# Expert layers: slots filled from one-hot products, token rows gathered tile by tile, shared tiles run beside the routing

## The reference, cut to what matters

```python
# expert layer 1 (F = 1024, 8 experts, best 2, with biases; the input rows are normalised first)
xn     = layernorm(x) * gamma + beta
probs  = softmax(xn @ Wr + br)
topv, topi = top_k(probs, 2)
moe    = sum over the two experts of  topv * (relu(xn @ W1[e] + b1[e]) @ W2[e] + b2[e])
# expert layer 2 (F = 512, 8 experts, best 2, no biases, weights renormalised) plus a shared expert for all tokens
probs  = softmax(xt @ Wg);  topv, topi = top_k(probs, 2);  topv = topv / sum(topv)
moe    = sum over the two experts of  topv * (gelu(xt @ Wu[e]) @ Wd[e])
shared = gelu(xt @ W1) @ W2
```

## Time and profile before

| | |
|---|---|
| median of 3 runs | 1692.89 us (1692.78 to 1692.92) |
| the profiled execution | 1693.18 us |
| its span | 1691.3 us |
| m0, first to last instruction | 686 to 1098 us of the span |
| m1 | 1407 to 1691 us of the span |
| PE, DVE, ACT, POOL busy | 84%, 66%, 60%, 56% |

### The profile page before, as it was taken

One profiled execution on the slowest core, in us unless ns is written; L12 is line 12 of the kernel. 1 busy time (PEld: TensorE's weight loads), 2 busy tenths in 40 slices (PEclk: granted clock), 3 DMA queues, 4 the chain that ended last, 5 costly groups with the idle time before them and its releaser, 6 DMA issues. The chain is left out here.

```text
span 1691.3 us, 28713 instructions
## 1 busy us (share of the span) xinstructions
PE 1412.6 (84%) x9650; PEld 1160.2 (69%) x9650; DVE 1115.1 (66%) x2456; ACT 1013.4 (60%) x2444; POOL 944.9 (56%) x940
## 2 busy tenths in 40 slices
PE   3778999999999999574999999168899965899991
PEld 3556777777777776564999999134555535789991
DVE  3566766666666666544677777569898962666664
ACT  3666565565565565103778788357777843358883
POOL 3786554444444445054888878127677761646661
PEclk9899999999999999586999999679999995899996
DMA  4100000000005600356565654254343410357664
GB/s 137 39 26 7 26 8 8 2 7 7 2 8 138 161 1 1 108 172 205 187 240 205 242 210 167 112 171 144 128 140 120 139 49 26 111 141 245 229 220 167
DMA packets 87453, 188.33 MB, mean 111 GB/s; under 512 B 25544, under 2 KB 58256, under 8 KB 78864
## 3 DMA queue, kind: packets, MB, share of 16 engines
q1 hardware_dynamic: 79824, 165.93, 29.5%
q0 software_dynamic: 7488, 20.59, 3.4%
HBM read 151.31 MB, written 35.18 MB: 110 GB/s over the span
## 5 line engine op out<-in xcount | busy, mean ns | idle before, releaser
L301 POOL TENSOR_TENSOR a_pexp<-a_pexp,a_rsum 128x384 f32<-128x384 f32 (+1 forms) x320 | 246.1, 787 | 282.5 <-DVE a_rsum L502 282.5
L394 ACT ACTIVATE a_pexp<-a_ps,a_nmax 128x384 f32<-128x384 f32 (+1 forms) x320 | 181.3, 568 | 175.3 <-DVE a_nmax L498 175.2
L1356 PE MATMUL m_ps<-m_xT,m_w1s 128*128 128x256 f32 x1848 | 279.4, 288 | 8.3 <-POOL m_w1s L841 5.1
L1374 PE MATMUL m_ps<-m_w2s,m_hs 128*128 128x256 f32 x1848 | 270.1, 282 | 2.7 <-DVE m_hs L1241 2.7
L1356 PEld LDWEIGHTS m_ps<-m_xT,m_w1s 128*128 128x128 f32 x1848 | 245.5, 193 | 13.9 <-POOL m_w1s L841 9.8
L1374 PEld LDWEIGHTS m_ps<-m_w2s,m_hs 128*128 128x128 f32 x1848 | 240.7, 189 | 3.1 <-DVE m_hs L1241 2.9
L498 DVE TENSOR_REDUCE a_nmax<-a_ps 128x1 f32<-128x384 f32 (+1 forms) x320 | 154.1, 523 | 68.3 <-PE a_ps L592 67.2
L1594 POOL TENSOR_TENSOR s_hc<-s_h,s_bc_rows 128x1024 f32<-128x1024 f32 x64 | 151.0, 2362 | 79.9 <-DVE s_h L1836 79.6
L841 POOL TENSOR_TENSOR m_w2s<-m_w,m_w2s 128x512 fp32r<-128x512 f32 x111 | 143.9, 1297 | 90.1 <-ACT m_w2s L1031 89.5
L1836 DVE TENSOR_TENSOR_SCAN s_h<-s_dps,s_inp 128x512 f32<-128x512 f32 x128 | 149.1, 1207 | 0.0
L608 PE MATMUL a_ps<-a_ident,a_pexp 128*128 128x128 f32 x896 | 145.1, 275 | 3.4 <-ACT a_pT L255 3.0
(11 more groups left out here) (318 smaller groups left out, 3269.1 us busy)
## 6 DMA issues: line engine op xcount, KB each, us to landing
s_bc_rows<-s_bc_table SPq DMA_DIRECT2D x64, 512.0 KB, 3.7
m_w<-in_down SPq DMA_DIRECT2D x31, 1024.0 KB, 8.2
m_w<-in_up SPq DMA_DIRECT2D x23, 1024.0 KB
m_w<-in_up SPq DMA_DIRECT2D x24, 512.0 KB
m_w<-in_down SPq DMA_DIRECT2D x24, 512.0 KB
slots<-a_zero SPq DMA_DIRECT2D x2, 5980.0 KB, 39.6
m_xrow<-slots SPq DMA_DIRECT2D x46, 256.0 KB
m_w<-results SPq DMA_DIRECT2D x4, 1024.0 KB, 7.8
```

The lines of the kernel that those rows point to most:

```text
L301: nc.gpsimd.tensor_tensor(pexp[:, r, 0:n], pexp[:, r, 0:n], rsum[:, r:r + 1].to_broadcast([128, n]), ALU.mult).then_inc(normed, 1)
L394: nc.scalar.activation(pexp[:, r, 0:n], ps_s[score_bank(u)][:, 0:n], ACT.Exp, bias=nmax[:, r:r + 1], accum_out=sums[:, r:r + 1]).then_inc( ...
L1356: last = nc.tensor.matmul(ps_hid[ft % RING], w1s[wb][wp][:, k, ft * 128:(ft + 1) * 128], xT[:, j % 2, xp, k, :], start=(k == 0 and wp == 0 ...
L1374: last = nc.tensor.matmul(ps_y[j % 2][:, s, :], hs[hp][:, ft % RING, s * 128:(s + 1) * 128], w2s[wb][wp][:, ft, :], start=(ft == 0 and s = ...
```

## The change

- The zero fill of the slot tables goes. Instead of `slots` there is a `table` of 2049 rows: row 0 is zero, row 1 + n is token n. SP stores the tokens' rows there by 4 plain DMAs of 4 blocks each.
- The 32 scatters go. The slot number is cut into a high digit (46 values) and a low one (128). DVE makes one-hot tables of both digits for the 32 (choice, block) pairs, and PE sums 32 products of them into the token number of every slot (`numbers_of_slots`). 64 more products give the weight of every slot (`weights_by_slot`); POOL prepares their right sides (`slot_weights`).
- The rows of a tile come by two indirect DMAs on POOL (`gather_rows`), those of tile j + 2 ahead of the other work of POOL's tile j. SP's `load_rows` goes.
- m1 starts its shared tiles right after the router scores. The routing is cut into steps that DVE does between them (`routing_step`), and PE's sums and products stand in the shared tiles 2, 6 and 7.
- m0: three of the eight constants run ahead of the sums, three between sums and products, two behind; x is doubled by ACT group by group in the routing, and the term is added by DVE in the tile loop, one block per tile.
- The chunks whose low part DVE makes are 0, 1, 2 (of 4) and 0, 3, 6 (of 8) in place of 0, 3 and 0, 4. In shared tiles ACT makes the rounded half of every hidden chunk.
- In m1 the rows of tiles 8 and 9 are transposed at step 0 of tiles 7 and 8 instead of step 2 of tiles 6 and 7.

```diff
-    on_dve = lambda c: c in (0, 3) if FT == 4 else c in (0, 4)
+    on_dve = lambda c: c in (0, 1, 2) if FT == 4 else c in (0, 3, 6)
+    high_on_act = lambda j, ft: j < TILES_SHARED or (ft % 4 in (1, 3) if FT == 4 else ft % 4 == 1)
...
+    def rows_at(j, ft):
+        if shared and ft == 0 and j + 1 in (TILES_SHARED, TILES_SHARED + 1):
+            return j + 1
+        if ft == X_STEP and j + 2 < TILES and not (shared and j + 2 in (TILES_SHARED, TILES_SHARED + 1)):
+            return j + 2
+        return None
...
 @block.sync
-                sp.wait_ge(s_scat, 16 * 2 * TT)
-                load_rows(TILES_SHARED)
-                load_rows(TILES_SHARED + 1)
+                for g in range(GROUPS):
+                    ...
+                    sp.dma_start(by_token[:, t, :], x[:, t, :] if ln_rows is None else xn_group(g)).then_inc(s_stored[g], 16)
...
 @block.gpsimd
-                for t in range(TT):
-                    for k in range(2):
-                        nc.gpsimd.indirect_dma_start(slots, ...(ap=slot_i[:, k, t:t + 1], axis=0), rows[:, t, :], None).then_inc(s_scat, 16)
+                def gather_rows(j):
+                    q, b = j - TILES_SHARED, j % 2
+                    pool.wait_ge(xT_raw, j + 1)
+                    for s in range(2):
+                        nc.gpsimd.indirect_dma_start(xrow[:, b, s, :], None, table,
+                                                     ...(ap=row_from[:, 2 * q + s:2 * q + s + 1], axis=0)).then_inc(xrow_loaded[b], 16)
...
+                if shared:
+                    slot_weights()
+                for g in range(GROUPS):
+                    pool.wait_ge(s_stored[g], 16)
+                pool.wait_ge(s_from, 1)
+                gather_rows(TILES_SHARED)
+                gather_rows(TILES_SHARED + 1)
                 if shared:
                     for c in range(FT):
                         low_part(TILES_SHARED, c)
+                else:
+                    slot_weights()
                 for j in range(TILES_SHARED, TILES):
+                    if j + 2 < TILES:
+                        gather_rows(j + 2)
                     if j == TILES_SHARED + 1:
                         destinations()
                     for c in range(FT):
                         if j + 1 < TILES:
                             low_part(j + 1, c)
                         if c == FT // 2 and j > TILES_SHARED:
                             scatter_rows(j - 1)
...
 @block.vector
+                def high_digits():
+                    link(nc.vector.tensor_tensor(high_hot[:], iota_hi..., slot_hi..., ALU.is_equal))   # 128 x 32 x 46
+                def numbers_by_high_digit():
+                    nc.vector.tensor_tensor(by_number[:], high_hot[:], value, ALU.mult).then_inc(s_by_number, 1)
+                def low_digits(c):                                                                   # 128 x 8 x 128
+                    nc.vector.tensor_tensor(low_hot[:, n, :], iota_lo..., slot_lo..., ALU.is_equal).then_inc(s_low_hot, 1)
...
 @block.tensor
+                def numbers_of_slots():
+                    pe.wait_ge(s_by_number, 1)
+                    for n in range(PAIRS):
+                        if n % (PAIRS // 4) == 0:
+                            pe.wait_ge(s_low_hot, n // (PAIRS // 4) + 1)
+                        last = nc.tensor.matmul(ps_id, low_hot[:, n, :], by_number[:, n, :], start=(n == 0), stop=(n == PAIRS - 1))
...
                 def transposes(j):
                     b, q = j % 2, j - TILES_SHARED
                     if routed(j):
-                        pe.wait_ge(xrow_loaded[b], 16 * (q // 2) + 16)
+                        pe.wait_ge(xrow_loaded[b], 32 * (q // 2) + 32)
...
+                        if shared and (j, ft) == (2, 1):
+                            count_slots()
+                        if shared and (j, ft) == (6, 1):
+                            numbers_of_slots()
+                        if (j, ft) == ((7, 1) if shared else (0, 4)):
+                            weights_by_slot()
+                        if rows_at(j, ft) is not None:
+                            transposes(rows_at(j, ft))
```

More of the change, by code:

```diff
@@ L284, in _ @@
                 for table in empty:
[L285 to L286 removed]
+                    sp.dma_start(table[0:1, :], zero[:]).then_inc(s_filled, 16)
                 sp.wait_ge(s_filled, 16 * len(empty))
@@ L1008, in take_root, with high_part @@
                     nc.scalar.activation(rstd[:, cols], rstd[:, cols], ACT.Sqrt).then_inc(s_rstd, 1)
+                W_DMAS = 3 if b_up is not None else 2
+                def high_part(weights, tile, c):
+                    n, half, wb = weights
+                    if c == 0:
+                        act_e.wait_ge(w_loaded[wb], (half + 1) * W_DMAS * 16)
+                        if tile is not None:
+                            act_e.wait_ge(h_used, tile * FT + 1)
+                    nc.scalar.copy(chunk(c, (w1s[wb][0], w2s[wb][0])), chunk(c, (w1[:, wb], w2[:, wb]))).then_inc(w_high, 1)
                 for g in range(GROUPS):
@@ L1248, in _ @@
                 dve.sem_inc(w_low_dve, 2 * DVE_LOWS)
+                if not shared:
+                    softmax_scores()
+                    probabilities()
+                    maxima()
+                    indices(0)
+                    indices(1)
+                    choices()
+                    one_hot()
+                    counts()
+                    tile_bounds()
+                    tile_experts()
+                    ranks()
+                    slot_numbers()
+                    slot_digits()
+                    high_digits()
+                    numbers_by_high_digit()
+                    for c in range(4):
+                        low_digits(c)
+                    slot_rows()
                 for c in range(FT):
@@ L2015, in decoder @@
     rows = (TOP_K * T + E * (SLOTS - 1)) // SLOTS * SLOTS
-    slots = [nc.dram_tensor(f"slots{n}", (rows, D + 4), fp32).ap() for n in range(2)]
-    results = [nc.dram_tensor(f"results{n}", (2 * T + 2 + rows, D), fp32).ap() for n in range(2)]
+    tables = [nc.dram_tensor(f"table{n}", (T + 1, D), fp32).ap() for n in range(2)]
+    results = [nc.dram_tensor(f"results{n}", (2 * T + rows, D), fp32).ap() for n in range(2)]
     flat = lambda t: t.rearrange("a s d -> (a s) d")
@@ L2037, in decoder @@
         moe_layer(nc, sems, "m1", tokens, flat(out), a["wr1"], None, None, a["up1"], None, a["down1"], None,
-                  slots[1], results[1], ACT.Gelu, True, True)
+                  tables[1], results[1], ACT.Gelu, True, True)
 def kernel(**inputs):
```

466 lines of the change are left out of this document (283 added, 183 removed).

## The result

| | time of the device | span of the profiled execution |
|---|---|---|
| kernel before | 1692.9 us (1692.8 to 1693.8, 4 runs) | 1691.3 us |
| predicted | 1736 us, range 1698 to 1776 | |
| changed kernel | 1886.5 us (1881.0 to 1889.3, 4 runs) | 1882.7 us |

The ratio is 1.114 (95% interval 1.111 to 1.117): slower, as forecast, but by 194 us instead of 43. The range didn't hold it, nor did the dearest rival (1774).

A forecast was written before the change was run, and what follows sets the result against it. PE was taken to bound the tile loops. From 1693.2 us, m0 gave -26, m1 ahead of tile 8 gave -1 and m1's routed tiles +70.6: 1736.8, or 1736 by the median's measure, range 1698 to 1776.

The forecast's parts named there:

- the dearest rival: m1's routed tiles: landing of 3.7 us and clock lost after each stall, 1774 us in all; chance 0.15.
- The chain in m1: m1's routed tiles: transposition, up, ACT, POOL's low part, gather, transposition close a loop; period 10.5 us, +70.6 in all.
- For L I take 3.0: m1's routed tiles: L, the gather's time from second DMA's issue to landing, taken as 3.0 us; period 9.98 before clock loss.
- In m0's loop the same chain has room: m0's tile loop: gather lands at X + 9.9 (X is a transposition), within a tile of 11.8 us, so no wait.
- lost in a third of the tiles: m1's routed tiles: PE's clock drops after the stall in a third of them, adding 0.5 us to the period.
- The rival with the clock always lost: The dearest rival: m1's clock lost after each stall, L = 3.7, tiles of 12.3 us, 1774 us in all; chance 0.15.
- The thin products: PE's added products of 46 columns at 0.09 us each: 5.8 us for 64 in m0, 8.6 for 96 in m1.
- The forecast's doubt: Sign that the prediction is wrong: products of 46 columns on PE costing more than 0.19 us each.
- m1's front: m1 ahead of tile 8: earlier start against added products, routing and first gather's wait; -1 us, ends -10 and +8.
- m0's loop starts at 758.6: m0's front: the loop's first transposition moves from 783.44 to 758.6, -24.8 us, within m0's total of -26.
- Rival 3: m1's routed tiles: gather hides behind PE because POOL comes early or the wait asks less; total near 1655 us; chance 0.10.
- Rival 4: m0's loop: indirect DMAs 0.2 us longer make POOL 12.0 us a tile, 13 us more, 1750 in all; chance 0.09.

The follow-up runs named there:

- e2: Changed kernel with each weight load cut to 128 KB from the third routed tile on, gathers left in place: 1795.1 us, 1.060 of before.
- e3: Changed kernel without POOL's gathers; SP loads rows of fixed positions by plain DMAs where it loaded rows before the change: 1698.0 us, 1.003 of before.
- e1: Changed kernel with POOL gathering the rows of tile j + 3 instead of j + 2, a tile earlier: 1714.1 us, 1.012 of before.
- e11: Changed kernel with SP issuing a tile's weights only when its rows have landed: 1829.6 us, 1.054 of before on its chip.
- e10: e1 plus 92-column weight products, reordered fronts, m0's addition moved a tile later, m1's chunk 2 low part ahead of DVE's split: 1683.5 us, 0.968 of before.

## Why the prediction was wrong

- **Right: the mechanism, link by link, and the sign.** The chain in m1 is as written. Its steps, as means of 20 tiles (T2 to T22, T10 to T30), beside the 11 tiles of e2's m1 in which the clock was kept:

| step of a period | forecast | m1 | m0 | e2, clock kept |
|---|---|---|---|---|
| transposition to POOL's low part | 4.15 + 0.5 | 5.97 | 4.66 | 4.20 |
| low part to first gather | 1.44 | 1.44 | 1.61 | 1.44 |
| first gather to second | 1.29 | 1.29 | 1.30 | 1.29 |
| second gather to next transposition (L + 0.1) | 3.1 | 4.43 | 6.87 | 3.04 |
| period | 10.5 | 13.1 | 14.4 | 9.98 |

  With the landing as forecast and no slow clock the period is 9.98, the forecast's own.
- **The failed step is "For L I take 3.0".** For the second DMA L is 4.4 in m1 and 6.8 in m0. e2, with small loads, has 3.3 and 3.4; the rest is the company of the weights. The text knew that the two start together, and its own rows had the price. The median of 3.7 in the earlier trace rows mixes two kinds. The first scatter of a pair leaves ahead of the weights, the second with them. In the kernel before, for the two scatters of the earlier trace rows, at 1557.59 and at 1558.88, and with SP's issue of the weights between them:

```profile
DMA to landing us min/median/max: 2.4/2.4/2.4
```

```profile
1558.83 0.33 SPq L891 DMA_DIRECT2D m_w<-in_down  x1
```

```profile
DMA to landing us min/median/max: 5.3/5.3/5.3
```

  Over the 18 pairs in 1520:1640 the first has a median of 2.4 and the second of 5.4, with 4.3 at the least. The bytes were in sight as well, 2.25 MB per tile of m0; at the 380 to 450 GB/s of the view above they are some 5.5 us. The Trainium skill ("DMA: Bandwidth & Descriptors", the anatomy of a DMA on the gpsimd path) gives 2.3 us, an estimate for one transfer by itself; e2's second gathers in m1 took 2.7 at the least and 3.0 in the median, so the rule was low even there.
- **"In m0's loop the same chain has room" fell with it.** It had 1.9 us (X + 9.9 against 11.8), and the landing took 3.7 more and the issue came 0.4 later: X + 13.9 in the median. The loop with twice the weights per tile had been given the same L. That is 51 of the missing 148 us.
- **The clock was taken as lost in a third of the tiles; in m1 it is lost in all 20** (granted clock 0.50 to 0.64 over the 3 us behind each transposition). The low part starts 1.8 us later than at the full clock, 1.3 more than the 0.5 counted; the landing is 1.3 over its 3.1. These two halves make the 2.6 us by which a period of 13.1 exceeds 10.5, 52 us in 20 tiles. The longer landing makes the longer stall, and no stall of 3.5 us or more kept the clock. The rival with the clock always lost had this half, but with L = 3.7 for its end, so 12.3.
- **The thin products.** Taken from transpositions, 0.09; measured 0.11, and 0.21 wherever they lowered the clock, so 9.8 and 13.5 us for 64. The nearer row was that of 423 products in 50 us, 0.12 each: products of 46, 92 and 256 columns cost much the same here. The forecast's doubt (over 0.19 each) came true in m1 and in half of m0's.
- **m1's front was 26 us over its 71.4.** 6.5 of them are a misreading: the 1494.69 of the earlier trace rows, taken as the start of tile 8 and of the old routed part, is the start of tile 7. Tile 8 starts at 1501.21, two steps ahead of the transposition at 1504.16. So the old routed part was 153.8 us and not 160.4, and the sum should have read +77 and 1743, still inside the range. The start itself came as forecast: T0 with the end of the scores. Added were 96 products in 19.9 us where 8.6 was counted, waits of 2.3 and 1.2 us behind VectorE's tables, 4.9 and 4.3 us of waiting for the first rows where 3.8 was counted, and slow products behind each.
- **VectorE's third low part and the addition were put at nothing.** e3, with no gather on POOL, has m1's tile at 7.1 instead of 6.8 and m0's long ones at 12.35.
- **Right: m0's loop starts at 758.6** (758.8). Of those 24.6 us, T0 to T2 took back 15.7.
- **Rival 3** is what e1 makes: POOL comes to the gather early. It gives 1714, not 1655, since the fronts are worse by 37 us than forecast (e1 has 1.6 at T0, 12.6 from T0 to T2, 23 in m1 with the 6.5 misread) and m1's tile stops at POOL's 7.0.
- **Rival 4**, POOL over in m0, isn't what happened: it is busy 37.5 of 50 us there, and its gathers take 0.98 us.

## What to carry to other kernels

When a transfer is moved, look at which event now releases it, and what else that event releases: price its landing from rows of transfers that were issued together with the same company, and look at whether a median mixes such with others. And when it stands in a closed chain with the engine that bounds the loop, take it out of the chain first (here three lines of order and no buffer gave back 172 of 194 us); keeping the weights out of its way gave 57 (e11), and with most of their bytes left out 91 (e2).

## What the hardware showed that was not expected

**DVE stands still while POOL multiplies.** The tables of 8 x 128 take DVE 1.21 us each, but in m1 the first two took 3.67 and 2.75, and PE waited 2.3 and 1.2 us behind them:

```profile
1514.28 2.66 POOL L987 TENSOR_TENSOR m_by_weight<-m_high_hot,m_wt_high 128x1472 fp32r<-128x1472 f32 x1 [24.70 <-DVE m_by_number L1271]
1517.02 3.52 POOL L987 TENSOR_TENSOR m_high_hot<-m_high_hot,m_wt_low 128x1472 fp32r<-128x1472 f32 x1
```

```profile
1514.35 3.67 DVE L1275 TENSOR_TENSOR m_low_hot<-m_iota_lo,m_slot_lo 128x1024 fp32r<-128x1024 f32 x1
...
1518.87 2.75 DVE L1275 TENSOR_TENSOR m_low_hot<-m_iota_lo,m_slot_lo 128x1024 fp32r<-128x1024 f32 x1
```

Each of DVE's ends 1.08 us after POOL's (1516.94 and 1518.02, 1520.54 and 1521.62): it was held until POOL was done. POOL's second multiplication, 3.52 us where the other three of its kind took 2.66, began inside the first table and was held in turn. The Trainium skill ("SBUF — State Buffer", who interferes with whom) says that a VectorE instruction with two on-chip inputs shuts out a GpSimd one that reads there, and the later one waits in full; the trace agrees. The prediction weighed only that page's warning for DMAs. The same two kinds of instruction meet in m0's loop, in the low parts: VectorE's took 0.68 to 0.70 us each before, and up to 3.3 in the changed kernel and 4.3 in e1 (e3's row above is one of them).

**Indirect issues on POOL last longer in a full loop.** Nearly all take 0.95 to 0.99 us in the changed kernel's m1; in e1's the gathers take 1.45 and 1.23, and in e10's the first of each pair 1.25 (gather) and 1.41 (scatter). Without that e10's POOL would need some 6.3 us a tile and not 7.0, an estimate from the changed kernel's rows above (1.45 + 3 x 1.29 + 0.97). No run isolates the cause.
